# A tile's down weights rounded and split in a step of its own, in a fused attention and mixture-of-experts kernel

## The chip, the cores and the metric

The kernel runs on one core of one Trainium2 chip. The metric is the device time of one execution in microseconds (us), the median of three runs.

## The reference

A cross-attention layer adds its result to `x` (4 batches of 1024 tokens, 256 wide), and then a mixture of 9 experts with 2 experts per token adds its own:

```python
x = x + _L0_xattn_ref(ctx_1024, _layernorm(x, axis=-1), fside_Bx16_0, fside_Bx16_0, ...)
x = x + _L0_ffn_ref(_layernorm(x, axis=-1), L0_ffn_Wr, L0_ffn_Wg, L0_ffn_Wu, L0_ffn_Wd)
```

The second line is the part in question. Each token goes through its two experts, of which each is a gated layer of 704 hidden columns:

```python
gate = jax.nn.silu(jnp.einsum('th,ehi->tei', xf, Wg))
hidden = gate * jnp.einsum('th,ehi->tei', xf, Wu)
out = jnp.einsum('tei,eih,te->th', hidden, Wd, cw)
```

## The kernel before

**Two halves.** Up to about 370 us the attention runs in steps of 128 tokens, and scatters every normalised token to the regions of its two experts in a DRAM table, `expert_in`. Then the experts run in 40 tiles. Tiles 0 to 2 (`EARLY`) are blocks of 256 rows of the expert with most rows. The others are 29 pairs (256 rows) and 8 singles (128 rows, tiles 6, 11, 16, 20, 25, 30, 34 and 39; `SINGLES_AFTER`). A step takes TensorE about 12 us for a pair (10.6 right behind a single) and 9.8 for a single, the down product of the tile before included.

**Split products.** fp32 products are made of three passes (`product`, lines 344 to 346): high part by high part, high by low, low by high. So every operand is split. ScalarE rounds the weights to `wgt_hi` (`round_pieces`, L1122), VectorE subtracts to get `wgt_lo` (`rest_pieces`, L1980). A tile has six pieces of weights (`PIECES`): four of 704 columns for gate and up, and for down one of 1280 columns and one of 256. The same holds for the tokens (`tok_move` L1107, `tok_rest` L1964) and for the hidden values (`hid_round` L1157 to L1160, `hid_rest` L2012 to L2016; for a single L1167 to L1170 and L2024 to L2027). `wgt_hi` and `wgt_lo` have two halves, used by turns.

**A step.** In step t, each engine works off a fixed list:

- TensorE: gate and up of tile t in three units (u = 0, 1, 2) of 256 hidden columns (the last of 192), each into a pair of PSUM banks, used by turns, so unit n waits until VectorE has read unit n-2 (`unit_free`, semaphore `hid_made`). After unit 1 it turns the tokens of tile t+1 (`tok_turn`, L1371), and then makes the down product of tile t-1 (`down`), which waits for the down weights of tile t-1, for its hidden values (`hid_ready`), and for bank space.
- ScalarE, for each unit: `silu`, two pieces of the weights of tile t+1, `hid_round`. After unit 1 also `tok_move(t + 1)` and `res_move(t - 1)`, which empties the down product of the tile before (L1179).
- VectorE, for each unit: `hidden` (gate times up, L1988 to L1991), two pieces of tile t+1, `hid_rest`. After unit 1 also `tok_rest(t + 1)`.

With u = 2 the two pieces are the down weights of tile t+1:

```python
                for u in range(UNITS):
                    hidden(t, u)
                    if t < NT - 1:
                        rest_pieces(t + 1, u, src)
                    hid_rest(t, u)
```

A single has one gate and up (`single_gate_up`), with its 128 tokens as the weights of the array and a hidden result that is turned (`hid_turn`, L1489 to L1492); in its step the four gate and up pieces of tile t+1 and the down product of t-1 all go by, and the down pieces of t+1 come last.

**Loads.** SyncE issues all loads. Pairs' raw weights lie in three slots (`wgt`) that are loaded three pairs ahead and only if the expert changes; a slot's number comes from a table in SBUF by `value_load`. Singles use `spare_wgt`. For each tile it loads the tokens of tile t+1, then refills the down weights behind tile t-1 and the gate and up weights behind tile t, each when VectorE has split the old ones.

**Results.** GpSimd notes the token numbers of tile t+2 (`note`, L930), then adds tile t's result to the output with indirect DMAs (`add_results`, L941), and waits until they have landed.

Of the kernel before, what the change touches and what calls it, by code (L numbers as in the profile page):

```python
# [28 lines left out]
P = 128  # L29
# [85 lines left out]
    return 0 if t < EARLY else t % 2  # L115


def pieces_to(t):

    return (t - EARLY) * len(PIECES)  # L120

def program(nc, x, ctx_rows, fside, ln1_w, ln1_b, ln2_w, ln2_b, wq, wkv, wout, wr, wg, wu, wd, out):
    valmat_dram = nc.dram_tensor("valmat_dram", (B, H, M, DE), F32).ap()
# [2 lines left out]
    with ExitStack() as ctx:  # L126
        def sem(name):
            return ctx.enter_context(nc.semaphore(name))
# [321 lines left out]
        tok_split = sem("tok_split")  # L450
        weights_hi = sem("weights_hi")
        weights_split = sem("weights_split")
        hid_made = sem("hid_made")
        hid_hi = sem("hid_hi")
        pads_zeroed = sem("pads_zeroed")
# [27 lines left out]
        def weights_loaded(t, gate_up):  # L483

            if not is_pair(t):
                return single_gu_loaded if gate_up else single_d_loaded, (TILES[t][1] + 1) * WEIGHT_LOADS
            pair = TILES[t][1]
            return (wgu_loaded if gate_up else wd_loaded)[pair % WEIGHT_SLOTS], (pair // WEIGHT_SLOTS + 1) * WEIGHT_LOADS

        def gate_up_split(t, u):  # L490

            return (early_split, u + 1) if t < EARLY else (weights_split, pieces_to(t) + 2 * KT)

        def down_split(t):
            return (early_split, UNITS + 2) if t < EARLY else (weights_split, pieces_to(t + 1))

        def tokens_loaded(t):
            return tok_loaded[t % 2], (t // 2 + 1) * 16
# [70 lines left out]
        def _(sp):  # L569
# [168 lines left out]
            def refill_gate_up(t):  # L738

                n = TILES[t][1]  # L740
                if is_pair(t) and n + WEIGHT_SLOTS < NP:
                    sp.wait_ge(weights_split, pieces_to(t) + 2 * KT)
                    load_pair_gate_up(n + WEIGHT_SLOTS)
                elif not is_pair(t) and n + 1 < NS:
                    sp.wait_ge(weights_split, pieces_to(t) + 2 * KT)
                    load_single_gate_up(n + 1)

            def refill_down(t):
                n = TILES[t][1]
                if is_pair(t) and n + WEIGHT_SLOTS < NP:  # L750
                    sp.wait_ge(weights_split, pieces_to(t + 1))
                    load_pair_down(n + WEIGHT_SLOTS)
                elif not is_pair(t) and n + 1 < NS:
                    sp.wait_ge(weights_split, pieces_to(t + 1))
                    load_single_down(n + 1)

            for t in range(EARLY, NT):
                if EARLY < t < NT - 1:
                    sp.wait_ge(tok_turned, t)
                    sp.wait_ge(tok_noted, t)  # L760
                    load_tokens(t + 1)
                if t > EARLY:
                    refill_down(t - 1)
                refill_gate_up(t)

            sp.wait_ge(added, BLOCKS_TO[NT] * 16)

# [189 lines left out]
        def _(act):  # L957
# [157 lines left out]

            def round_pieces(t, u, src):

                act.wait_ge(*weights_loaded(t, u < UNITS - 1))
                if u == UNITS - 1 and t > EARLY:
                    act.wait_ge(down_done, t - 1)  # L1120
                for p0, p1 in PIECES[2 * u:2 * u + 2]:
                    nc.scalar.activation(wgt_hi[half_of(t)][:, p0:p1], src[:, p0:p1], ACT.Copy).then_inc(weights_hi, 1)  # L1122

            def early_round(u):

# [56 lines left out]
            def pair_step(t):  # L1182

                ahead = EARLY - 1 <= t < NT - 1
                src = weights_of(t + 1) if ahead else None
                for u in range(UNITS):
                    silu(t, u)
                    if ahead:
                        round_pieces(t + 1, u, src)
                    hid_round(t, u)  # L1190
                    if u == UNITS - 2 and t:
                        tok_move(t + 1)
                        if t == 2:
                            act.wait_ge(last_stored, 16)
                        res_move(t - 1)

            def single_step(t):

                last = t == NT - 1
                src = None if last else weights_of(t + 1)  # L1200
                single_silu(t)
                if not last:
                    round_pieces(t + 1, 0, src)
                    tok_move(t + 1)
                    round_pieces(t + 1, 1, src)
                res_move(t - 1)
                single_hid_round(t)
                if not last:
                    round_pieces(t + 1, 2, src)

            for s in range(T + 4):
                step(s, s)
# [328 lines left out]
        def _(dve):  # L1541
# [431 lines left out]
            def rest_pieces(t, u, src):  # L1973

                i = t % 2
                for n in range(2 * u, 2 * u + 2):
                    p0, p1 = PIECES[n]
                    rows = P if n < len(PIECES) - 1 else FHALF
                    dve.wait_ge(weights_hi, pieces_to(t) + n + 1)
                    nc.vector.tensor_tensor(wgt_lo[i][0:rows, p0:p1], src[0:rows, p0:p1],  # L1980
                                            wgt_hi[i][0:rows, p0:p1].bitcast(F32), ALU.subtract).then_inc(weights_split, 1)

            def hidden(t, u):

# [45 lines left out]
            def pair_step(t):  # L2030

                src = weights_of(t + 1) if t < NT - 1 else None
                for u in range(UNITS):
                    hidden(t, u)
                    if t < NT - 1:
                        rest_pieces(t + 1, u, src)
                    hid_rest(t, u)
                    if t < NT - 1 and u == UNITS - 2:
                        tok_rest(t + 1)

            def single_step(t):

                last = t == NT - 1
                src = None if last else weights_of(t + 1)
                single_hidden(t)
# [61 lines left out]
```

## Time and profile before

| what | value |
|---|---|
| median of 3 runs | 832.52 us (832.21 to 832.76) |
| the profiled execution | 832.81 us, of which the span of its instructions is 831.2 us |
| mean granted TensorE clock | 0.996 |
| TensorE busy | 795.7 us (96%) |
| VectorE, ScalarE, GpSimd busy | 667.6, 625.8, 380.2 us |

The rows below come from the one profiled execution. Times in the timeline count from the start of its span. A row says when an instruction starts, how long it takes, its engine and line, what it writes and reads, and in brackets how long the engine stood idle before it and whose work ended that. Matmuls overlap: the next one starts 0.11 to 0.12 us after a 256-column one that is listed with 0.28 us.

### The profile page before, as it was taken

The page shows a single profiled execution, that of the slowest core. Times are in us where ns is not written, and L with a number is a line of the kernel's source. Part 1 is how long each engine was busy: PE and PEld are TensorE (multiplying, and loading weights), DVE is VectorE, ACT ScalarE, POOL GpSimd, SP SyncE. Part 2 cuts the span into 40 slices and gives each one's busy share as a digit, 9 for nine tenths or more (in the row PEclk, how much of TensorE's full clock was granted, in tenths as well). Part 3 has the DMA queues.
Part 4 walks back from the last instruction along what each step waited for, and adds up shares of the span by engine and source line. Part 5 has one row for each costly group of instructions (what it writes and reads, how often), then busy time and mean ns, then how long its engine had stood idle before and what let it go on. Part 6 is the DMA issues. An engine that isn't in the chain of part 4 may idle for free.

```text
span 831.2 us, 19592 instructions
## 1 busy us (share of the span) xinstructions
PE 795.7 (96%) x6037; PEld 754.9 (91%) x6037; DVE 667.6 (80%) x1620; ACT 625.8 (75%) x1966; POOL 380.2 (46%) x534
## 2 busy tenths in 40 slices
PE   7999999999999999879999999999999999999993
PEld 6866999999999999779999999999999999999993
DVE  6778888888888887887878788787888877888771
ACT  4578898889889888655777778777778777777771
POOL 3021377688778767763334233442343424424232
PEclk9999999999999999999999999999999999999998
DMA  8065900401310020656575182255752654556211
GB/s 288 20 152 147 268 32 30 150 27 40 122 52 33 33 85 27 210 155 171 148 199 120 25 262 46 47 170 152 225 153 46 194 159 119 133 142 160 40 23 23
DMA packets 78044, 96.14 MB, mean 116 GB/s; under 512 B 10680, under 2 KB 65140, under 8 KB 77940
## 3 DMA queue, kind: packets, MB, share of 16 engines
q1 hardware_dynamic: 64179, 75.94, 29.7%
q0 software_dynamic: 13760, 18.96, 12.4%
q8 instruction: 48, 0.79, 0.4%
q14 instruction: 57, 0.46, 0.2%
HBM read 108.14 MB, written 31.29 MB: 168 GB/s over the span
## 4 chain that ended last, share of the span: by engine, by line
PE 82%; DVE 4%; issue 3%; SPq 3%; POOL 2%; DMA 2%; ACT 2%; DVEq 1%; POOLq 0%
PE banks L344 23%; PE banks L345 22%; PE banks L346 22%; PE banks L1357 4%; PE banks L1337 2%; PE banks L1514 2%; PE banks L1371 2%; PE banks L1311 1%; DMA expert_in<-blank 1%; POOL expert_in L878 1%; PE banks L1287 1%; ACT prob L1046 1%; DVEq L1544 1%; PE banks L1323 1%; SPq L657 1%
## 5 line engine op out<-in xcount | busy, mean ns | idle before, releaser
L344 PE MATMUL banks<-tok_t_hi,wgt_hi 128*128 128x256 f32 x704 | 199.7, 284 | 4.8 <-DVE hid_f L1988 1.9
L346 PE MATMUL banks<-tok_t_hi,wgt_lo 128*128 128x256 f32 x704 | 198.0, 281 | 0.0
L345 PE MATMUL banks<-tok_t_lo,wgt_hi 128*128 128x256 f32 x704 | 197.9, 281 | 0.0
L941 POOL DMA_INDIRECT result<-res,tok_id x72 | 117.7, 1635 | 161.2 <-ACT res L1179 129.9
L1046 ACT ACTIVATE prob<-banks,row_min 128x77 f32<-128x77 f32 x512 | 161.8, 375 | 2.9 <-DVE row_min L1711 2.9
L1980 DVE TENSOR_TENSOR wgt_lo<-wgt,wgt_hi 128x704 fp32r<-128x704 f32 x174 | 150.4, 905 | 14.7 <-ACT wgt_hi L1122 14.7
L344 PEld LDWEIGHTS banks<-tok_t_hi,wgt_hi 128*128 128x128 f32 x704 | 134.3, 191 | 7.9 <-issue 5.9
L346 PEld LDWEIGHTS banks<-tok_t_hi,wgt_lo 128*128 128x128 f32 x704 | 133.5, 190 | 0.0
L345 PEld LDWEIGHTS banks<-tok_t_lo,wgt_hi 128*128 128x128 f32 x704 | 133.4, 189 | 0.0
L1122 ACT ACTIVATE wgt_hi<-wgt 128x704 fp32r (+1 forms) x174 | 130.6, 801 | 0.5
L1046 ACT ACTIVATION_READ_ACCUMULATOR prob<-banks,row_min 128x1 f32 x512 | 131.0, 257 | 0.0
L344 PE MATMUL banks<-wgt_hi,hid_hi 128*128 128x256 f32 x360 | 104.3, 290 | 8.7 <-issue 6.1
L346 PE MATMUL banks<-wgt_hi,hid_lo 128*128 128x256 f32 x360 | 101.3, 281 | 0.0
L345 PE MATMUL banks<-wgt_lo,hid_hi 128*128 128x256 f32 x360 | 101.1, 281 | 0.0
L344 PE MATMUL banks<-valmat_hi,prob_t_hi 128*128 128x266 f32 x320 | 94.5, 295 | 1.0 <-DVE logits L1733 1.0
L891 POOL TENSOR_TENSOR prob<-prob,row_inv 128x1232 f32<-128x1232 f32 x32 | 72.1, 2254 | 50.9 <-DVE row_inv L1725 50.9
L345 PE MATMUL banks<-valmat_lo,prob_t_hi 128*128 128x266 f32 x320 | 91.6, 286 | 0.0
L346 PE MATMUL banks<-valmat_hi,prob_t_lo 128*128 128x266 f32 x320 | 91.5, 286 | 0.0
L878 POOL DMA_INDIRECT expert_in<-xn,top_slot x64 | 67.4, 1053 | 39.0 <-POOL xn L868 24.9
L930 POOL COPY tok_gate<-tok 128x2 f32<-128x2 f32 (+1 forms) x40 | 23.9, 598 | 131.8 <-DMA result<-res,tok_id 128.6
L344 PEld LDWEIGHTS banks<-wgt_hi,hid_hi 128*128 128x128 f32 x360 | 68.3, 190 | 10.9 <-DVE wgt_lo L1980 6.0
L1061 ACT ACTIVATE prob_t_hi<-banks 128x512 fp32r<-128x512 f32 (+1 forms) x96 | 48.8, 543 | 33.0 <-PE banks L1357 33.0
(274 smaller groups left out, 2131.3 us busy)
## 6 DMA issues: line engine op xcount, KB each, us to landing
wgt<-in_L_ffn_Wg SPq DMA_DIRECT2D x29, 704.0 KB
wgt<-in_L_ffn_Wu SPq DMA_DIRECT2D x29, 640.0 KB
wgt<-in_L_ffn_Wd SPq DMA_DIRECT2D x29, 640.0 KB
tok<-expert_in SPq DMA_DIRECT2D x32, 258.0 KB, 3.4
spare_wgt<-in_L_ffn_Wg SPq DMA_DIRECT2D x9, 704.0 KB, 4.2
spare_wgt<-in_L_ffn_Wu SPq DMA_DIRECT2D x9, 640.0 KB, 5.9
spare_wgt<-in_L_ffn_Wd SPq DMA_DIRECT2D x9, 640.0 KB, 4.3
valmat_f<-valmat_dram SPq DMA_DIRECT2D x4, 1197.0 KB, 6.3
```

The source lines that it names most:

```text
L344: nc.tensor.matmul(to, a[0], b[0], start=first, stop=False)
L345: nc.tensor.matmul(to, a[0], b[1], start=False, stop=False)
L346: return nc.tensor.matmul(to, a[1], b[0], start=False, stop=last)
L878: nc.gpsimd.indirect_dma_start(expert_in, bass.IndirectOffsetOnAxis(ap=top_slot[c % 4][:, k:k + 1], axis=0), xn[c % 4][:, k, :], None).the ...
L891: nc.gpsimd.tensor_tensor(p, p, row_inv[i][:].unsqueeze(2).to_broadcast([P, H, M]), ALU.mult).then_inc(prob_ready, 1)
L930: nc.gpsimd.tensor_copy(tok_gate[:, t % NOTES, 0:blocks], tok[i][:, 0:blocks, GATE])
L941: nc.gpsimd.indirect_dma_start(out, bass.IndirectOffsetOnAxis(ap=tok_id[:, t % NOTES, a:a + 1], axis=0), res[i][:, a, :], None, compute_op ...
L1046: ins = nc.scalar.activation(prob[c % 2][:, h * M:(h + 1) * M], bank[i][:, (h - h0) * M:(h - h0 + 1) * M], ACT.Exp, bias=row_min[c % 2][:, ...
L1061: ins = nc.scalar.activation(prob_t[c % 2][0][0:rows, m0:m1, :], turned_bank(c, g, rows, m0 - c0, m1 - c0), ACT.Copy)
L1122: nc.scalar.activation(wgt_hi[half_of(t)][:, p0:p1], src[:, p0:p1], ACT.Copy).then_inc(weights_hi, 1)
L1357: mm = nc.tensor.transpose(bank[3 + (c * NG + g) % 2][0:n, (m - c0) * P:(m - c0 + 1) * P], prob[c % 2][:, m * P:m * P + n], ident[:])
L1980: nc.vector.tensor_tensor(wgt_lo[i][0:rows, p0:p1], src[0:rows, p0:p1], wgt_hi[i][0:rows, p0:p1].bitcast(F32), ALU.subtract).then_inc(weig ...
```

## The change

The two down pieces leave `round_pieces` and `rest_pieces`. They get functions of their own, `round_down` and `rest_down`, and semaphores of their own, `down_hi` and `down_split_made`. The down weights of a pair t are now rounded and split in step t, right behind the turned tokens of tile t+1, no longer in step t-1 behind unit 2. For a single t they are made at the end of step t, at the place where those of tile t+1 stood; for the last tile, ahead of its `res_move` and `single_hid_rest`. In exchange, ScalarE and VectorE look up a pair's slot twice, for t+1 and for t. On SyncE the gate and up refill of tile t now comes before the down refill behind tile t-1.

```diff
-def pieces_to(t):
+def gate_pieces_to(t):
-    return (t - EARLY) * len(PIECES)
+    return (t - EARLY) * 2 * KT
+def down_pieces_to(t):
+    return (t - EARLY) * (len(PIECES) - 2 * KT)
...
         def down_split(t):
-            return (early_split, UNITS + 2) if t < EARLY else (weights_split, pieces_to(t + 1))
+            return (early_split, UNITS + 2) if t < EARLY else (down_split_made, down_pieces_to(t + 1))
...
             for t in range(EARLY, NT):
                 if EARLY < t < NT - 1:
                     sp.wait_ge(tok_turned, t)
                     sp.wait_ge(tok_noted, t)
                     load_tokens(t + 1)
+                refill_gate_up(t)
                 if t > EARLY:
                     refill_down(t - 1)
-                refill_gate_up(t)
...
             def round_pieces(t, u, src):
-                act.wait_ge(*weights_loaded(t, u < UNITS - 1))
-                if u == UNITS - 1 and t > EARLY:
-                    act.wait_ge(down_done, t - 1)
+                act.wait_ge(*weights_loaded(t, True))
                 for p0, p1 in PIECES[2 * u:2 * u + 2]:
                     nc.scalar.activation(wgt_hi[half_of(t)][:, p0:p1], src[:, p0:p1], ACT.Copy).then_inc(weights_hi, 1)
+            def round_down(t, src):
+                act.wait_ge(*weights_loaded(t, False))
+                if t > EARLY:
+                    act.wait_ge(down_done, t - 1)
+                for p0, p1 in PIECES[2 * KT:]:
+                    nc.scalar.activation(wgt_hi[half_of(t)][:, p0:p1], src[:, p0:p1], ACT.Copy).then_inc(down_hi, 1)
...
                 src = weights_of(t + 1) if ahead else None
+                own = weights_of(t) if t >= EARLY else None
                 for u in range(UNITS):
                     silu(t, u)
-                    if ahead:
+                    if ahead and u < UNITS - 1:
                         round_pieces(t + 1, u, src)
                     hid_round(t, u)
                     if u == UNITS - 2 and t:
                         tok_move(t + 1)
+                        if t >= EARLY:
+                            round_down(t, own)
                         if t == 2:
                             act.wait_ge(last_stored, 16)
                         res_move(t - 1)
...
+                if last:
+                    round_down(t, spare_wgt[:])
                 res_move(t - 1)
                 single_hid_round(t)
                 if not last:
-                    round_pieces(t + 1, 2, src)
+                    round_down(t, spare_wgt[:])
...
+            def rest_down(t, src):
+                i = t % 2
+                for n, (p0, p1) in enumerate(PIECES[2 * KT:]):
+                    rows = FHALF if n else P
+                    dve.wait_ge(down_hi, down_pieces_to(t) + n + 1)
                     nc.vector.tensor_tensor(wgt_lo[i][0:rows, p0:p1], src[0:rows, p0:p1],
-                                            wgt_hi[i][0:rows, p0:p1].bitcast(F32), ALU.subtract).then_inc(weights_split, 1)
+                                            wgt_hi[i][0:rows, p0:p1].bitcast(F32), ALU.subtract).then_inc(down_split_made, 1)
...
                 for u in range(UNITS):
                     hidden(t, u)
-                    if t < NT - 1:
+                    if t < NT - 1 and u < UNITS - 1:
                         rest_pieces(t + 1, u, src)
                     hid_rest(t, u)
-                    if t < NT - 1 and u == UNITS - 2:
-                        tok_rest(t + 1)
+                    if u == UNITS - 2:
+                        if t < NT - 1:
+                            tok_rest(t + 1)
+                        if t >= EARLY:
+                            rest_down(t, own)
...
+                if last:
+                    rest_down(t, spare_wgt[:])
                 single_hid_rest(t)
                 if not last:
-                    rest_pieces(t + 1, 2, src)
+                    rest_down(t, spare_wgt[:])
```

VectorE's list in the first pair step whose next tile is a single, from the turned tokens of the single to the first products of its hidden values. Before (`L1980` are the down pieces of the single, `L2015` and `L2016` are `hid_rest` of the pair's unit 2, `L1971` is the look-up of a slot):

```order
L1964 TENSOR_TENSOR tok_t_lo<-banks,tok_t_hi 128x2x128 [waits tok_moved]
L1990 TENSOR_TENSOR hid_f<-gate_act,banks 128x256 [waits silu_done]
L1991 TENSOR_TENSOR hid_f<-gate_act,banks 64x256
L1980 TENSOR_TENSOR wgt_lo<-spare_wgt,wgt_hi 128x1280 [waits weights_hi]
L1980 TENSOR_TENSOR wgt_lo<-spare_wgt,wgt_hi 64x256 [waits weights_hi]
L2015 TENSOR_TENSOR hid_lo<-hid_f,hid_hi 128x256 [waits hid_hi]
L2016 TENSOR_TENSOR hid_hi<-hid_f,hid_hi 64x256
L1971 TENSOR_LOAD tile_table
L1971 ISA x2
L2000 TENSOR_TENSOR single_hid<-single_act,banks 128x256 [waits silu_done]
L2001 TENSOR_TENSOR single_hid<-single_act,banks 128x64
```

Now (`L2005` are the down pieces of the pair itself, its `ISA` rows compute the slot's address, `L2040` and `L2041` are `hid_rest`, and `L1988` is the look-up):

```order
L1981 TENSOR_TENSOR tok_t_lo<-banks,tok_t_hi 128x2x128 [waits tok_moved]
L2005 ISA [waits down_hi]
L2005 TENSOR_TENSOR wgt_lo<-wgt,wgt_hi 128x1280
L2005 ISA [waits down_hi]
L2005 TENSOR_TENSOR wgt_lo<-wgt,wgt_hi 64x256
L2015 TENSOR_TENSOR hid_f<-gate_act,banks 128x256 [waits silu_done]
L2016 TENSOR_TENSOR hid_f<-gate_act,banks 64x256
L2040 TENSOR_TENSOR hid_lo<-hid_f,hid_hi 128x256 [waits hid_hi]
L2041 TENSOR_TENSOR hid_hi<-hid_f,hid_hi 64x256
L1988 TENSOR_LOAD tile_table
L1988 ISA x2
L2025 TENSOR_TENSOR single_hid<-single_act,banks 128x256 [waits silu_done]
```

The two down pieces have moved from between `hidden` and `hid_rest` of unit 2 to ahead of that `hidden`; `hid_rest` now follows `hidden` directly.

ScalarE's list at the same place. Before (`L1122` are the down pieces of the single, `L1179` empties the down product of the tile before, `L1146` and `L1147` are `silu` of unit 2, `L1159` and `L1160` are `hid_round`):

```order
L1107 ACTIVATE tok_t_hi<-banks 128x2x128 [waits tok_turned]
L1179 ACTIVATE res<-banks,tok_gate 128x256 [waits added,tok_noted,down_done]
L1179 ACTIVATE res<-banks,tok_gate 128x256
L1146 ACTIVATE gate_act<-banks 128x256 [waits gu_done]
L1147 ACTIVATE gate_act<-banks 64x256
L1122 ACTIVATE wgt_hi<-spare_wgt 128x1280 [waits down_done,single_d_loaded]
L1122 ACTIVATE wgt_hi<-spare_wgt 128x256
L1159 ACTIVATE hid_hi<-hid_f 128x256 [waits hid_made]
L1160 ACTIVATE hid_hi<-hid_f 64x256
```

Now (`L1134` are the down pieces of the pair itself, `L1191` empties the down product):

```order
L1113 ACTIVATE tok_t_hi<-banks 128x2x128 [waits tok_turned]
L1134 ISA [waits down_done,wd_loaded2]
L1134 ACTIVATE wgt_hi<-wgt 128x1280
L1134 ISA
L1134 ACTIVATE wgt_hi<-wgt 128x256
L1191 ACTIVATE res<-banks,tok_gate 128x256 [waits added,tok_noted,down_done]
L1191 ACTIVATE res<-banks,tok_gate 128x256
L1158 ACTIVATE gate_act<-banks 128x256 [waits gu_done]
L1159 ACTIVATE gate_act<-banks 64x256
L1171 ACTIVATE hid_hi<-hid_f 128x256 [waits hid_made]
L1172 ACTIVATE hid_hi<-hid_f 64x256
```

The rounding of the down pieces has moved from between `silu` and `hid_round` of unit 2 to between the turned tokens and the emptying of the down product. TensorE's list has not changed.

## Rows read from the trace of the kernel before

**Rows 1.** The page, busy time, share of the span, instructions
```profile
PE 795.7 (96%) x6037; PEld 754.9 (91%) x6037; DVE 667.6 (80%) x1620; ACT 625.8 (75%) x1966; POOL 380.2 (46%) x534
```

**Rows 2.** Waits, 400 to 831 us: total us, times, longest
```profile
PEld banks L344 <- DVE wgt_lo L1980: 7.0, 12, 1.3
PE banks L344 <- issue: 6.8, 11, 2.0
```

**Rows 3.** Timeline, TensorE, start of down products in single steps
```profile
436.19 0.35 PE L344 MATMUL banks<-wgt_hi,hid_hi 128*128 128x256 f32 x1 [0.59 <-issue]
...
492.18 0.60 PE L1371 MATMUL banks<-ident,tok 128*128 128x128 f32 x4
493.34 0.36 PE L344 MATMUL banks<-wgt_hi,hid_hi 128*128 128x256 f32 x1 [0.56 <-issue]
...
811.20 0.36 PE L344 MATMUL banks<-wgt_hi,hid_hi 128*128 128x256 f32 x1 [0.99 <-DVE wgt_lo L1980]
```

**Rows 4.** Timeline, VectorE, around the second single
```profile
486.86 0.42 DVE L1964 TENSOR_TENSOR tok_t_lo<-banks,tok_t_hi 128x256 fp32r<-128x256 f32 x1
489.34 0.42 DVE L1990 TENSOR_TENSOR hid_f<-gate_act,banks 128x256 f32<-128x256 f32 x1 [2.07 <-ACT gate_act L1147]
489.78 0.42 DVE L1991 TENSOR_TENSOR hid_f<-gate_act,banks 64x256 f32<-64x256 f32 x1
490.64 1.82 DVE L1980 TENSOR_TENSOR wgt_lo<-spare_wgt,wgt_hi 128x1280 fp32r<-128x1280 f32 x2 [0.45 <-ACT wgt_hi L1122]
...
492.82 0.42 DVE L2016 TENSOR_TENSOR hid_hi<-hid_f,hid_hi 64x256 fp32r<-64x256 f32 x1
...
496.41 1.68 DVE L1980 TENSOR_TENSOR wgt_lo<-wgt,wgt_hi 128x704 fp32r<-128x704 f32 x2
```

**Rows 5.** Timeline, ScalarE, around the second single
```profile
485.31 0.36 ACT L1107 ACTIVATE tok_t_hi<-banks 128x256 fp32r<-128x256 f32 x1
486.39 0.84 ACT L1179 ACTIVATE res<-banks,tok_gate 128x256 f32<-128x256 f32 x2 [0.72 <-PE banks L1514]
488.53 0.39 ACT L1146 ACTIVATE gate_act<-banks 128x256 f32<-128x256 f32 x1 [1.31 <-PE banks L346]
...
489.33 1.59 ACT L1122 ACTIVATE wgt_hi<-spare_wgt 128x1280 fp32r<-128x1280 f32 x2
...
491.13 0.41 ACT L1160 ACTIVATE hid_hi<-hid_f 64x256 fp32r<-64x256 f32 x1
```

**Rows 6.** Timeline, the pair step after the first single, by engine
```profile
443.39 1.82 DVE L1980 TENSOR_TENSOR wgt_lo<-wgt,wgt_hi 128x1280 fp32r<-128x1280 f32 x2 [0.39 <-ACT wgt_hi L1122]
445.14 0.67 DVE L1988 TENSOR_TENSOR hid_f<-gate_act,banks 128x512 f32<-128x512 f32 x1
...
450.75 0.67 DVE L1964 TENSOR_TENSOR tok_t_lo<-banks,tok_t_hi 128x512 fp32r<-128x512 f32 x1
...
452.58 0.42 DVE L1991 TENSOR_TENSOR hid_f<-gate_act,banks 64x256 f32<-64x256 f32 x1
...
449.66 0.47 ACT L1179 ACTIVATE res<-banks,tok_gate 128x256 f32<-128x256 f32 x1
451.34 0.39 ACT L1146 ACTIVATE gate_act<-banks 128x256 f32<-128x256 f32 x1 [1.21 <-PE banks L346]
...
451.52 0.35 PE L344 MATMUL banks<-tok_t_hi,wgt_hi 128*128 128x256 f32 x1 [0.22 <-issue]
```

**Rows 7.** Line L1971, VectorE's look-up of a slot: ns min/median/max, first and last start
```profile
L1971 DVEq TENSOR_LOAD <-tile_table x28: 300/304/550, 396.8 to 785.0; - x28
L1971 DVEq FUSED_REGOPS  x28: 190/190/216, 397.4 to 785.4; - x28
```

**Rows 8.** Timeline, the end: GpSimd adds the result of tile 38
```profile
817.18 1.56 POOL L941 DMA_INDIRECT result<-res,tok_id  x1 [7.88 <-ACT res L1179]
```

**Rows 9.** Timeline, tokens: TensorE waits for a tile's; SyncE issues a later one's
```profile
412.48 0.66 PE L1371 MATMUL banks<-ident,tok 128*128 128x128 f32 x4 [0.31 <-DMA tok<-expert_in]
...
502.40 0.39 SPq L668 DMA_DIRECT2D tok<-expert_in  x1
```

More of the change, by code:

```diff
@@ L452, in program @@
         weights_split = sem("weights_split")
+        down_hi = sem("down_hi")
+        down_split_made = sem("down_split_made")
         hid_made = sem("hid_made")
@@ L490, in gate_up_split @@
         def gate_up_split(t, u):
-            return (early_split, u + 1) if t < EARLY else (weights_split, pieces_to(t) + 2 * KT)
+            return (early_split, u + 1) if t < EARLY else (weights_split, gate_pieces_to(t + 1))
         def down_split(t):
-            return (early_split, UNITS + 2) if t < EARLY else (weights_split, pieces_to(t + 1))
+            return (early_split, UNITS + 2) if t < EARLY else (down_split_made, down_pieces_to(t + 1))
         def tokens_loaded(t):
@@ L741, in refill_gate_up @@
                 if is_pair(t) and n + WEIGHT_SLOTS < NP:
-                    sp.wait_ge(weights_split, pieces_to(t) + 2 * KT)
+                    sp.wait_ge(weights_split, gate_pieces_to(t + 1))
                     load_pair_gate_up(n + WEIGHT_SLOTS)
                 elif not is_pair(t) and n + 1 < NS:
-                    sp.wait_ge(weights_split, pieces_to(t) + 2 * KT)
+                    sp.wait_ge(weights_split, gate_pieces_to(t + 1))
                     load_single_gate_up(n + 1)
@@ L750, in refill_down @@
                 if is_pair(t) and n + WEIGHT_SLOTS < NP:
-                    sp.wait_ge(weights_split, pieces_to(t + 1))
+                    sp.wait_ge(down_split_made, down_pieces_to(t + 1))
                     load_pair_down(n + WEIGHT_SLOTS)
                 elif not is_pair(t) and n + 1 < NS:
-                    sp.wait_ge(weights_split, pieces_to(t + 1))
+                    sp.wait_ge(down_split_made, down_pieces_to(t + 1))
                     load_single_down(n + 1)
@@ L1977, in rest_pieces @@
                     p0, p1 = PIECES[n]
-                    rows = P if n < len(PIECES) - 1 else FHALF
-                    dve.wait_ge(weights_hi, pieces_to(t) + n + 1)
+                    dve.wait_ge(weights_hi, gate_pieces_to(t) + n + 1)
+                    nc.vector.tensor_tensor(wgt_lo[i][:, p0:p1], src[:, p0:p1], wgt_hi[i][:, p0:p1].bitcast(F32), ALU.subtract
+                                            ).then_inc(weights_split, 1)
+            def rest_down(t, src):
[3 more added lines that the diff above has]
+                    dve.wait_ge(down_hi, down_pieces_to(t) + n + 1)
                     nc.vector.tensor_tensor(wgt_lo[i][0:rows, p0:p1], src[0:rows, p0:p1],
-                                            wgt_hi[i][0:rows, p0:p1].bitcast(F32), ALU.subtract).then_inc(weights_split, 1)
+                                            wgt_hi[i][0:rows, p0:p1].bitcast(F32), ALU.subtract).then_inc(down_split_made, 1)
             def hidden(t, u):
@@ L2032, in pair_step @@
                 src = weights_of(t + 1) if t < NT - 1 else None
+                own = weights_of(t) if t >= EARLY else None
                 for u in range(UNITS):
                     hidden(t, u)
-                    if t < NT - 1:
+                    if t < NT - 1 and u < UNITS - 1:
                         rest_pieces(t + 1, u, src)
                     hid_rest(t, u)
-                    if t < NT - 1 and u == UNITS - 2:
-                        tok_rest(t + 1)
+                    if u == UNITS - 2:
[3 more added lines that the diff above has]
+                            rest_down(t, own)
             def single_step(t):
```

## The prediction

> **What bounds the kernel now.** First the page: TensorE is busy for 96% of the span [rows 1], and at full clock, so only its gaps can be won, unless work leaves it, and none does. Then the waits of the expert half, where all edits lie: TensorE's own waits for VectorE's weight pieces and "issue" come to 7.0 us in front of weight loads and 6.8 us in front of matmuls [rows 2]. The two count the same gaps twice, so some 8 us is all there is. Then the timeline of TensorE, to see where the gaps are. In plain pair steps there is none. In each of the 8 single steps the down product of the pair before starts late: 0.59 us idle at 436.19, 0.56 at 493.34, 0.99 at 811.20 [rows 3]; the other five (550, 595, 652, 709, 754) show 0.56 once and 0.59 four times. Measured from start to start it is 0.16 more, since a matmul is listed 0.28 us long where the next starts after 0.12: the four turned-token matmuls at 492.18 take 4 x 0.11 us, so the down product was due at 492.62, and came at 493.34, 0.72 late [rows 3].
>
> Who ends that wait? The view names the weights or "issue". The down product waits for its weights (made a step earlier), bank space (long free), and the pair's last hidden values. VectorE's list shows the third: `hidden` of unit 2 is done at 489.78 + 0.42 = 490.20, then the two down pieces of the single run from 490.64, and only then `hid_rest` ends at 492.82 + 0.42 = 493.24, 0.10 before TensorE starts [rows 4]. So VectorE does 1.75 us of work for a later product, after 0.45 of waiting for ScalarE's rounding, ahead of what TensorE wants now.
>
> **The change part by part.** *Taken out from between `hidden` and `hid_rest`: two subtractions on VectorE and two roundings on ScalarE.* ScalarE may round the hidden values when `hidden` is done at 490.20. Its two instructions took from about 490.8 to 491.13 + 0.41 [rows 5], some 0.7 us, so they end near 490.95, and `hid_rest`'s two (0.86 us, [rows 4]) near 491.9. TensorE comes at 492.62. Margin 0.7 us: the wait goes whole. Seven times 0.74 (0.56 to 0.59 plus 0.16) is 5.2 us, the last one 0.99 + 0.16 = 1.15. **Sum 6.3 us.** Behind the last one, GpSimd's adds start from ScalarE's emptying of that very down product [rows 8], so the end of the span moves with it.
>
> *Put in, behind the turned tokens.* VectorE stands idle for 2.07 us there, from 487.28 to `hidden` at 489.34 [rows 4]; the two pieces fill 1.75 of it. ScalarE has two holes, 0.72 before it empties the down product and 1.31 before unit 2's `silu` [rows 5]; the roundings (1.5 us) fit into 2.03, though the emptying starts some 0.8 later, for which only GpSimd's adds wait (TensorE needs that bank a step later). I cost this at nothing. If the cover were gone, `hidden` of unit 2 would slip, and TensorE's unit 1 of the next step waits for it, one unit (2.9 us) after the end of unit 2.
>
> *The step behind a single is the tight one,* since VectorE has no hole: from the down pieces at 443.39 to the turned tokens at 450.75 + 0.67 it is busy, and TensorE waits for these, 0.22 idle at 451.52 [rows 6]. The change leaves that chain as it is: it starts from the end of the down product, and as many pieces of the same sizes lie in it. So TensorE cannot win there what it saves elsewhere in the same step, and this gap stays. Behind the tokens, the down pieces now run from 451.35 to 453.10, and `hidden` of unit 2 ends at about 453.95, where it was 452.58 + 0.42 = 453.00 [rows 6]. TensorE's next unit 1 is due 24 matmuls x 0.12 after 451.52, at 454.4. Margin 0.4 us: nothing lost. If it slips further, seven steps pay.
>
> *The second look-up of a slot,* in 28 pair steps on ScalarE and on VectorE. One is a load of 0.30 and register work of 0.19, from 785.0 to about 785.6, so 0.6 us of the sequencer [rows 7]. It runs while the engine still works off what it was given. In plain steps there is room. Behind a single it must fit beside the down pieces: two look-ups, 1.2 us, against the 1.75 us from 443.39 to 445.14 [rows 6]. Bounds: nothing, or all of it in seven steps, 7 x 0.6 = 4.2 us. I take nothing, by the room of 1.75.
> The Trainium skill, page "DMA: Bandwidth & Descriptors", section "Latency and other measured facts", gives a `tensor_load` a floor of about 0.6 us. With that figure two look-ups would take 1.8 us, and together with the hand-over of the pieces some 0.3 us would show in each of seven steps, an estimate of 2.1 us given back, so 828.3 us. The trace has 0.30 [rows 7] and does not agree, and I go by the trace.
>
> *SyncE.* Its list is as long as before. The down refill now waits for pieces made later, and the tokens of the tile after next stand behind both refills. Around a single they were issued at 502.40 [rows 9]; I expect 3 us later. They are needed by TensorE's turn at about 514, two steps on. If they came late, it would look as at 412.48, 0.31 us idle [rows 9]; that one, before the first changed refill, stays. Cost nothing. The loads of weights are needed three pairs later, as before.
>
> **Sum.** Own time 832.81 us less 6.3 is 826.5. The profiled execution lies 0.29 over the median, so the median should come to **826.2 us**. No more than 0.2% (1.7 us) apart counts as no change.
>
> **Rivals.**
> 1. *Part is given back behind the singles.* The emptier list shows new waits: the look-ups (up to 4.2 us), or unit 1's wait for `hidden` of unit 2, whose margin of 0.4 us is made of estimates; each 0.3 us over it costs 7 x 0.3 = 2.1. For it: VectorE is saturated there. Against: both have rows with room. Time 828 to 830.5. The floor for a load on the page of the Trainium skill named above ("DMA: Bandwidth & Descriptors") is this rival's case of 828.3 us; of its chance I give that 0.03, since 28 loads of 0.30 speak against it.
> 2. *The gap isn't the hidden values'.* "Issue" in [rows 3] could be TensorE's own, when it turns to other weights. Then nothing moves: 832.5. Against: the start follows `hid_rest` by 0.10 us, and where no turned tokens come before (811.20) the gap is longer by just their 0.4.
> 3. *Slower: `hidden` of unit 2 becomes late in every pair step.* The place is VectorE's hole behind the turned tokens. The down pieces now stand ahead of `hidden` and wait for ScalarE's rounding and for the loaded weights. Their room is the 2.07 us hole and 1.2 us more: unit 1 is due 2.9 us after unit 2's end, of which `silu` takes 0.8 and `hidden` 0.86. Beyond that TensorE waits in each of 28 steps. It decides from 3.3 us on, against 1.75 measured [rows 4]. At 3.8 us it would cost 28 x 0.5 = 14 us, less the 6.3: 840. Against: it needs the pieces to take twice their time.
> 4. *More is won.* If the gaps behind singles (0.22 idle, [rows 6], up to 0.38 from start to start, seven of them) went too, some 2 us more: 824.
>
> **How the numbers follow.** Forecast (825.4 to 827.2) 0.72, rival 1 0.11, rival 2 0.05, rival 3 0.05, rival 4 0.07. The likeliest gives 826.2. The range goes down to 824.8, for part of rival 4 and my 0.2 us a step, and up to 829.2, for most of rival 1; what is left out is rivals 2 and 3, the end of rival 1 and half of rival 4, under 0.2. Faster by over 0.2% is the forecast, rival 4 and nearly all of rival 1: 0.89, and I take off a little for what I have not thought of: 0.87. Within 0.2%: 0.07. Slower: 0.06.
>
> **What would show it.** In the profile after: TensorE's down product follows the turned tokens in single steps without a gap, all eight times; VectorE's `hid_rest` directly behind `hidden` and ScalarE's rounding; the two down pieces in VectorE's hole behind the turned tokens, and the idle time before `hidden` of unit 2 (2.07) down to about 0.3; the emptying of the down product about 0.8 us later than TensorE's end; the gap of 0.2 behind singles still there; tokens issued 3 us later without a wait on them. The prediction is wrong if a gap stays in front of the down product, if TensorE waits in front of unit 1 in plain pair steps, or if the look-ups show as idle time before unit 0's `silu` or `hidden` with TensorE behind them.

## The result, and the profile after

The changed kernel takes 825.71 us, median of 4 executions (825.07 to 826.43), where the kernel before took 832.52. The ratio is 0.9918 (95% interval 0.9906 to 0.993): 6.8 us less, where 6.3 were forecast. The profiled execution took 826.43 us with a span of 824.8 (before: 831.2).

The page of the changed kernel, busy time and share of the span, answers to [rows 1]:

```profile
PE 792.2 (96%) x6037; PEld 755.3 (92%) x6037; DVE 670.0 (81%) x1620; ACT 625.4 (76%) x1966; POOL 382.7 (46%) x534
```

The counts of instructions are the same, so no engine does less work; only gaps went. TensorE's busy time is 3.5 us less all the same, because a matmul is listed 0.28 us long where the next one can start after 0.12: the first part of each gap counts as busy. The waits of the changed kernel, 400 to 825 us (engine, line waited for: us in total, times, longest), answer to [rows 2]:

```profile
DVE hid_f L2015 <- ACT gate_act L1159: 23.6, 22, 1.3
DVE hid_lo L2040 <- ACT hid_hi L1172: 23.0, 29, 0.8
...
PEld banks L348 <- issue: 5.6, 8, 2.3
...
PE banks L348 <- issue: 4.1, 7, 2.0
```

The wait for `wgt_lo` in front of a product has left the list. Of the 4.1 us, 2.0 is the very last down product's. Where the rest is, TensorE's timeline shows (L1388 turns tokens, L1506 to L1509 turn a single's hidden values, L348 begins a product; it answers to [rows 3], [rows 6] and [rows 9]):

```profile
412.77 0.60 PE L1388 MATMUL banks<-ident,tok 128*128 128x128 f32 x4
...
450.85 0.35 PE L348 MATMUL banks<-tok_t_hi,wgt_hi 128*128 128x256 f32 x1 [0.29 <-issue]
...
491.50 0.60 PE L1388 MATMUL banks<-ident,tok 128*128 128x128 f32 x4
491.85 0.36 PE L348 MATMUL banks<-wgt_hi,hid_hi 128*128 128x256 f32 x1
...
496.55 0.27 PE L1509 MATMUL banks<-ident,single_hid 128*64 128x128 f32 x1
496.58 0.36 PE L348 MATMUL banks<-tok_t_hi,wgt_hi 128*128 128x256 f32 x1
```

The down product at 491.85 starts 0.35 us after the token turn at 491.50, where it took 493.34 - 492.18 = 1.16 [rows 3]. All eight of these gaps are gone. Another gain was not forecast. From the turn of a single's hidden values to the next gate product TensorE took 0.74 us five times and 0.65 twice before, now 0.57 to 0.59 each time, 1.0 us over seven singles. The gaps behind the singles grew: from start to start 0.38, 0.18, 0.38, 0.18, 0.18, 0.38, 0.19 (1.9 us) became 0.45, 0.17, 0.72, 0.47, 0.39, 0.56, 0.48 (3.2 us). The gaps in front of the down products were 5.8 us over seven singles and 1.1 at the last, so the balance is 5.8 + 1.1 + 1.0 - 1.4 = 6.5 us. A count without any model of gaps gives 6.7: from the turn of tile 5's tokens to the start of the last down product, TensorE takes 405.7 us before (412.48 to 818.20) and 399.0 now (412.77 to 811.74). The whole span is only 6.4 us shorter, since the changed kernel's profiled execution was already 0.8 us late at a token turn at 343.29 (before: 342.49), ahead of every changed step; 0.5 of that came back, as it did not have the token wait of [rows 9].

VectorE in the changed kernel around the second single (L2005 are the two down pieces, L2015 and L2016 `hidden` of unit 2, L2040 and L2041 `hid_rest`, L1996 pieces of the next tile's gate and up weights), to lay beside [rows 4]:

```profile
485.01 0.42 DVE L1981 TENSOR_TENSOR tok_t_lo<-banks,tok_t_hi 128x256 fp32r<-128x256 f32 x1
485.57 1.82 DVE L2005 TENSOR_TENSOR wgt_lo<-wgt,wgt_hi 128x1280 fp32r<-128x1280 f32 x2
488.66 0.42 DVE L2015 TENSOR_TENSOR hid_f<-gate_act,banks 128x256 f32<-128x256 f32 x1 [1.27 <-ACT gate_act L1159]
489.10 0.42 DVE L2016 TENSOR_TENSOR hid_f<-gate_act,banks 64x256 f32<-64x256 f32 x1
490.31 0.42 DVE L2040 TENSOR_TENSOR hid_lo<-hid_f,hid_hi 128x256 fp32r<-128x256 f32 x1 [0.79 <-ACT hid_hi L1172]
490.75 0.42 DVE L2041 TENSOR_TENSOR hid_hi<-hid_f,hid_hi 64x256 fp32r<-64x256 f32 x1
...
494.59 1.68 DVE L1996 TENSOR_TENSOR wgt_lo<-wgt,wgt_hi 128x704 fp32r<-128x704 f32 x2
```

And ScalarE there (L1134 rounds the down pieces, L1191 empties the down product), beside [rows 5]:

```profile
484.13 1.58 ACT L1134 ACTIVATE wgt_hi<-wgt 128x1280 fp32r x2
485.71 0.84 ACT L1191 ACTIVATE res<-banks,tok_gate 128x256 f32<-128x256 f32 x2
487.86 0.39 ACT L1158 ACTIVATE gate_act<-banks 128x256 f32<-128x256 f32 x1 [1.31 <-PE banks L350]
...
489.55 0.42 ACT L1171 ACTIVATE hid_hi<-hid_f 128x256 fp32r<-128x256 f32 x1 [0.92 <-DVE hid_f L2016]
```

The hidden values are ready at 490.75 + 0.42 = 491.17, 0.68 us ahead of the product. Both engines now wait in front of `hid_rest` for each other's previous step instead of working on weights.

### The profile page after: what moved, and what is told of

Its sections match the earlier page's. It is cut to its first block, busy times and chain, and to the rows that moved or that the text cites. A ratio compares the mean times of both kernels' runs of the same rounds, so it can differ in the third digit from the quotient of the medians.

```text
span 824.8 us, 19760 instructions
## 1 busy us (share of the span) xinstructions
PE 792.2 (96%) x6037; PEld 755.3 (92%) x6037; DVE 670.0 (81%) x1620; ACT 625.4 (76%) x1966; POOL 382.7 (46%) x534
## 4 chain that ended last, share of the span: by engine, by line
PE 87%; DVE 5%; ACT 2%; issue 1%; DVEq 1%; POOL 1%; DMA 1%; SPq 0%; POOLq 0%
PE banks L348 25%; PE banks L349 24%; PE banks L350 24%; PE banks L1374 4%; PE banks L1354 2%; PE banks L1531 2%; PE banks L1388 2%; PE banks L1328 1%; DVEq L1561 1%; PE banks L1304 1%; ACT prob L1052 1%; PE banks L1340 1%; DMA wkv_sb<-in_L_xattn_Wkv 0%; DMA result<-res,tok_id 0%; DVE prob_t_lo L1703 0%
## 5 line engine op out<-in xcount | busy, mean ns | idle before, releaser
L348 PE MATMUL banks<-tok_t_hi,wgt_hi 128*128 128x256 f32 x704 | 200.3, 285 | 5.1 <-issue 2.5
L947 POOL DMA_INDIRECT result<-res,tok_id x72 | 119.4, 1658 | 144.9 <-ACT res L1191 111.6
L348 PEld LDWEIGHTS banks<-tok_t_hi,wgt_hi 128*128 128x128 f32 x704 | 135.0, 192 | 6.9 <-issue 6.0
L348 PE MATMUL banks<-wgt_hi,hid_hi 128*128 128x256 f32 x360 | 104.2, 290 | 3.5 <-issue 2.0
L1996 DVE TENSOR_TENSOR wgt_lo<-wgt,wgt_hi 128x704 fp32r<-128x704 f32 x116 | 97.8, 884 | 0.6 <-issue 0.2
L348 PE MATMUL banks<-valmat_hi,prob_t_hi 128*128 128x266 f32 x320 | 94.4, 295 | 0.9 <-DVE logits L1750 0.9
L1126 ACT ACTIVATE wgt_hi<-wgt 128x704 fp32r (+1 forms) x116 | 84.9, 784 | 0.0
L936 POOL COPY tok_gate<-tok 128x2 f32<-128x2 f32 (+1 forms) x40 | 20.6, 515 | 138.4 <-DMA result<-res,tok_id 138.4
L348 PE MATMUL banks<-keymat_hi,zn_t_hi 128*128 128x462 f32 (+1 forms) x192 | 72.7, 379 | 0.0
```

The costliest lines, as they stand in the source:

```text
L348: nc.tensor.matmul(to, a[0], b[0], start=first, stop=False)
L936: nc.gpsimd.tensor_copy(tok_gate[:, t % NOTES, 0:blocks], tok[i][:, 0:blocks, GATE])
L947: nc.gpsimd.indirect_dma_start(out, bass.IndirectOffsetOnAxis(ap=tok_id[:, t % NOTES, a:a + 1], axis=0), res[i][:, a, :], None, compute_op ...
L1996: nc.vector.tensor_tensor(wgt_lo[i][:, p0:p1], src[:, p0:p1], wgt_hi[i][:, p0:p1].bitcast(F32), ALU.subtract).then_inc(weights_split, 1)
```

## The experiments

The theory: the down product waited for `hid_rest`, which stood behind the pieces. Its rivals: the gap belongs to TensorE; or the gain has another source in the change. x1 to x4 ran beside 15 executions of the kernel before (median 832.61), x5 to x8 beside 12 (832.71). Ratios are to those.

**x1_put_back.** The changed kernel with everything as it is (functions, semaphores, two look-ups, the refill order), but a pair's own down pieces made between `silu` and `hid_round`, and between `hidden` and `hid_rest`, of its unit 2:

```diff
+                    if t >= EARLY and u == UNITS - 1:
+                        round_down(t, own)
                     hid_round(t, u)
...
-                        if t >= EARLY:
-                            round_down(t, own)
...
+                    if t >= EARLY and u == UNITS - 1:
+                        rest_down(t, own)
                     hid_rest(t, u)
...
-                        if t >= EARLY:
-                            rest_down(t, own)
```

> The changed kernel, with the down pieces of a pair's own tile put back between `hidden` and `hid_rest` of unit 2 (VectorE) and between `silu` and `hid_round` (ScalarE); own semaphores, second look-up and the new refill order stay. Theory (the gain is the hidden values' wait in single steps): the gap in front of the down product comes back eight times, 0.7 to 0.8 us each and 1.2 at the last, so 832 us, within 1 us of the kernel before (832.52). Rival (the gain comes from the new refill order or the semaphores): it stays near 825.7.

Measured: 833.9 us (11 executions), ratio 1.0016 (1.0007 to 1.0025). The whole gain is gone, with 1.3 us more. Timeline of x1, VectorE's down pieces and TensorE's down products:

```profile
433.89 1.82 DVE L2005 TENSOR_TENSOR wgt_lo<-wgt,wgt_hi 128x1280 fp32r<-128x1280 f32 x2 [0.56 <-ACT wgt_hi L1134]
...
436.58 0.36 PE L348 MATMUL banks<-wgt_hi,hid_hi 128*128 128x256 f32 x1 [0.71 <-issue]
...
812.90 0.36 PE L348 MATMUL banks<-wgt_hi,hid_hi 128*128 128x256 f32 x1 [1.11 <-DVE wgt_lo L2005]
```

All eight gaps are back, each 0.12 us longer than before (0.71 for 0.59, 1.11 for 0.99, [rows 3]); VectorE waits 0.56 us for the rounding where it waited 0.45 [rows 4]. That is 1.0 of the 1.3 us. So the place of the pieces carries the gain; the rest of the change brings none by itself. That the extra 0.11 is the slot's address, which both engines now work out here, was not measured apart.

**x2_rounding_moved_only.** From the changed kernel; ScalarE rounds early as in the change, VectorE still splits between `hidden` and `hid_rest`:

```diff
+                    if t >= EARLY and u == UNITS - 1:
+                        rest_down(t, own)
                     hid_rest(t, u)
...
-                        if t >= EARLY:
-                            rest_down(t, own)
```

> ScalarE rounds the down pieces at the new place, VectorE subtracts them at the old one, ahead of `hid_rest`. Theory: VectorE no longer waits 0.45 us for the rounding, but its 1.75 us of work still lie ahead, so `hid_rest` ends some 0.3 us after the down product is due (0.7 at the last): gaps of 0.3 x 7 + 0.7 = 2.8 us, 828.5 us. Rival (VectorE's wait for ScalarE was the cost): all of the gain stays, 825.7.

Measured: 829.14 us (5 executions), ratio 0.9963 (0.9949 to 0.9976), about half of the gain. Timeline of x2, VectorE around the second single, then two of TensorE's down products:

```profile
488.81 1.82 DVE L2005 TENSOR_TENSOR wgt_lo<-wgt,wgt_hi 128x1280 fp32r<-128x1280 f32 x2
490.55 0.41 DVE L2040 TENSOR_TENSOR hid_lo<-hid_f,hid_hi 128x256 fp32r<-128x256 f32 x1
...
434.86 0.35 PE L348 MATMUL banks<-wgt_hi,hid_hi 128*128 128x256 f32 x1 [0.18 <-issue]
...
807.11 0.36 PE L348 MATMUL banks<-wgt_hi,hid_hi 128*128 128x256 f32 x1 [0.57 <-issue]
```

VectorE's wait of 0.45 us for the rounding is gone, and the seven gaps shrink from 0.59 idle to 0.18, the last from 0.99 to 0.57, 0.42 each: 3.3 us, close to the 3.5 measured. The other half needs VectorE's own 1.75 us out of the way, and so does the 1.0 us at the next gate product: from the turn of a single's hidden values to that product TensorE takes 0.74 us five times and 0.65 twice in x2, as before. It also speaks against the rival that the gap is TensorE's own: TensorE's list is the same in x1, x2 and the change, and the gap has three sizes.

**x5_hidden_first.** From the kernel *before*: nothing leaves its step; only the order within unit 2 is turned, `hid_round` and `hid_rest` ahead of the pieces.

```diff
-                    if ahead:
+                    if ahead and u < UNITS - 1:
                         round_pieces(t + 1, u, src)
                     hid_round(t, u)
+                    if ahead and u == UNITS - 1:
+                        round_pieces(t + 1, u, src)
...
-                    if t < NT - 1:
+                    if t < NT - 1 and u < UNITS - 1:
                         rest_pieces(t + 1, u, src)
                     hid_rest(t, u)
+                    if t < NT - 1 and u == UNITS - 1:
+                        rest_pieces(t + 1, u, src)
```

> The kernel before, with only this turned round in unit 2 of a pair step: `hid_round` and `hid_rest` come first, then the two down pieces of the next tile. Theory: the gap in front of the down product goes, but VectorE then does the 1.75 us of pieces ahead of the single's own products and pieces, so gate and up of the tile behind the single waits instead (some 1 us in each of seven); the gain is lost there but for the last single: 832.5 us, within 1 us. Rival (whatever gets the pieces out of the way of `hid_rest` gives the whole gain): 826.

Measured: 835.19 us (8 executions), ratio 1.0031 (1.002 to 1.0041): slower than before, though the gap that the prediction was about is gone. Timeline of x5, VectorE and then TensorE (L1982 are weight pieces, L2017 is `hid_rest`, L1373 turns tokens):

```profile
491.41 0.43 DVE L2017 TENSOR_TENSOR hid_lo<-hid_f,hid_hi 128x256 fp32r<-128x256 f32 x1 [0.79 <-ACT hid_hi L1160]
...
492.57 1.82 DVE L1982 TENSOR_TENSOR wgt_lo<-spare_wgt,wgt_hi 128x1280 fp32r<-128x1280 f32 x2 [0.31 <-ACT wgt_hi L1122]
...
497.56 1.68 DVE L1982 TENSOR_TENSOR wgt_lo<-wgt,wgt_hi 128x704 fp32r<-128x704 f32 x2
...
492.59 0.60 PE L1373 MATMUL banks<-ident,tok 128*128 128x128 f32 x4
492.95 0.36 PE L344 MATMUL banks<-wgt_hi,hid_hi 128*128 128x256 f32 x1
...
499.30 0.39 PE L344 MATMUL banks<-tok_t_hi,wgt_hi 128*128 128x256 f32 x1 [1.38 <-DVE wgt_lo L1982]
```

The down product starts on time (0.36 after the turn), and TensorE stands 1.38 us in front of the next tile's gate product, for weight pieces that end at 497.56 + 1.68 = 499.24. It does so in all seven singles that a pair follows, 1.38 to 1.49 us each, 10.2 in all. The kernel before had this limit too, hidden by the first gap. Its timeline of TensorE:

```profile
498.03 0.27 PE L1492 MATMUL banks<-ident,single_hid 128*64 128x128 f32 x1
498.14 0.39 PE L344 MATMUL banks<-tok_t_hi,wgt_hi 128*128 128x256 f32 x1
```

The pieces it needs ended at 496.41 + 1.68 = 498.09 [rows 4], 0.05 ahead of it, and in the other six singles the distance is the same. So VectorE's list from `hidden` of unit 2 to the last gate piece set the pace of the single step, with the gap only showing where. In x5 that list is longer by its waits, 0.79 + 0.31 for 0.45: from the start of `hidden` to the end of the pieces 9.48 us (489.76 to 499.24) for 8.75 (489.34 to 498.09). The changed kernel has 494.59 + 1.68 - 488.66 = 7.61, as the down pieces no longer lie in it. The expectation had the place of the stall right and its size too small.

**x3_one_lookup.** From the changed kernel; the slot's number that step t-1 read for t is kept, not read again:

```diff
+            looked_up = {}
...
-                src = weights_of(t + 1) if ahead else None
-                own = weights_of(t) if t >= EARLY else None
+                own = looked_up.get(t)
+                src = looked_up[t + 1] = weights_of(t + 1) if ahead else None
...
-                src = None if last else weights_of(t + 1)
+                src = looked_up[t + 1] = None if last else weights_of(t + 1)
```

> The changed kernel with one look-up of a slot per step: the register of the step before is used again. Theory (look-ups are mostly covered): VectorE shows 0.19 us of 'issue' in front of unit 0's `hidden` behind one single, and the gaps behind singles grew by 1.4 us in all, of which 1.0 is TensorE's earlier arrival; so 0.4 us less than the changed kernel, a ratio to before of about 0.9913. Rival (a load's floor of about 0.6 us, as a page of the notes gives it): 2 us less, ratio 0.9895.

Measured: 824.93 us (5 executions), ratio 0.9911 (0.9897 to 0.9924), against 0.9913 (0.99 to 0.9927) of the changed kernel run again (x8): not told apart by the times. The trace does tell: the gaps behind singles sum to 2.6 us from start to start (0.45, 0.17, 0.44, 0.44, 0.18, 0.44, 0.47), for 3.2 in the changed kernel. By this the second look-up costs some 0.6 us (0.5 against x8, whose gaps sum to 3.1). Its rows in the changed kernel (VectorE's sequencer, then ScalarE's; min/median/max in ns) and the one place where it shows in front of VectorE's `hidden` of unit 0:

```profile
L1988 DVEq TENSOR_LOAD <-tile_table x56: 298/306/659, 397.0 to 791.5; - x56
```

```profile
L1120 ACTq TENSOR_LOAD <-tile_table x56: 272/280/602, 396.3 to 790.8; - x56
```

```profile
557.21 0.69 DVE L2013 TENSOR_TENSOR hid_f<-gate_act,banks 128x512 f32<-128x512 f32 x1 [0.19 <-issue]
```

The median load is 0.31 us. The floor of about 0.6 us in the Trainium skill ("DMA: Bandwidth & Descriptors", "Latency and other measured facts") is reached by three of VectorE's 56 loads and one of ScalarE's 56, so the measured median decides; the case of 828.3 us that rested on it did not come.

**x4_single_early.** From the changed kernel; in single steps too the down pieces are made ahead of `res_move` and `single_hid_round`, and on VectorE ahead of `single_hid_rest`, as the change does for the last tile alone:

```diff
-                if last:
-                    round_down(t, spare_wgt[:])
+                round_down(t, spare_wgt[:])
                 res_move(t - 1)
                 single_hid_round(t)
-                if not last:
-                    round_down(t, spare_wgt[:])
...
-                if last:
-                    rest_down(t, spare_wgt[:])
+                rest_down(t, spare_wgt[:])
                 single_hid_rest(t)
-                if not last:
-                    rest_down(t, spare_wgt[:])
```

> The changed kernel; in every single step (not only the last) the single's own down pieces come ahead of the emptying of the down product and of `single_hid_rest`, in the time in which ScalarE (1.54 us) and VectorE (1.03 us) wait for TensorE. Theory (TensorE's gap behind singles is VectorE's chain from there to the turned tokens): VectorE is 0.5 us earlier at unit 0's `hidden`, the seven gaps of 0.17 to 0.72 us (3.2 in all) shrink to under 0.3 in all, and the time is 822.8 us, ratio 0.988. Rival (the gap is set by ScalarE or by the tokens' turn): no change, 825.7.

Measured: 822.99 us (4 executions), ratio 0.9886 (0.9871 to 0.9901). Timeline of x4, VectorE in the first single step (L2002 are the single's down pieces, L2046 is `single_hid_rest`):

```profile
439.29 1.81 DVE L2002 TENSOR_TENSOR wgt_lo<-spare_wgt,wgt_hi 128x1280 fp32r<-128x1280 f32 x2
441.02 0.68 DVE L2046 TENSOR_TENSOR hid_lo<-banks,hid_hi 128x512 fp32r<-128x512 f32 x1
...
443.18 0.69 DVE L2010 TENSOR_TENSOR hid_f<-gate_act,banks 128x512 f32<-128x512 f32 x1 [0.99 <-ACT gate_act L1156]
```

VectorE now waits 0.99 us for the next unit 0, where it came late, and none of TensorE's starts behind a single is later by more than 0.12. The gap behind singles is the same kind of gap as the first: weights for later, standing ahead of what is wanted now.

**x6_old_refill_order.** From the changed kernel, with the down refill again ahead of the gate and up refill:

```diff
-                refill_gate_up(t)
                 if t > EARLY:
                     refill_down(t - 1)
+                refill_gate_up(t)
```

> The changed kernel with the refills in the old order (down behind tile t-1 first, then gate and up behind tile t). Theory: loads have two or three steps of room, so no change: 825.7, within 0.5 us. Rival (the order matters): over 1 us slower.

Measured: 827.05 us (5 executions, 826.96 to 827.61), ratio 0.9934 (0.9921 to 0.9948), where x8 beside it took 825.65 (825.19 to 825.72): 1.4 us slower. That is the rival's case ("over 1 us slower"), not the theory's. Timeline of x6, SyncE's loads and TensorE's turn:

```profile
657.99 0.37 SPq L661 DMA_DIRECT2D spare_wgt<-in_L_ffn_Wd  x1
...
661.81 0.39 SPq L654 DMA_DIRECT2D wgt<-in_L_ffn_Wg  x1
...
664.87 0.38 SPq L674 DMA_DIRECT2D tok<-expert_in  x1
...
670.29 0.66 PE L1388 MATMUL banks<-ident,tok 128*128 128x128 f32 x4 [1.02 <-DMA tok<-expert_in]
```

And the same place in x8, the changed kernel:

```profile
654.25 0.39 SPq L654 DMA_DIRECT2D wgt<-in_L_ffn_Wg  x1
...
657.56 0.38 SPq L661 DMA_DIRECT2D spare_wgt<-in_L_ffn_Wd  x1
...
660.54 0.39 SPq L674 DMA_DIRECT2D tok<-expert_in  x1
...
668.86 0.60 PE L1388 MATMUL banks<-ident,tok 128*128 128x128 f32 x4
```

In both, the down refill waits until the down pieces are split (in x6 they end at 657.25). The gate and up loads were through before that in x8; in x6 they stand behind it, and the tokens behind them go out 4.3 us later and land after TensorE asks for them: 1.02 us idle here. With a second, smaller one at 569.15 it is 1.4 us from start to start. From tile 5's turn to the last down product TensorE takes 400.1 us in x6 and 398.8 in x8. So the refill order is no ornament: with pieces made later, the old order would give back 1.4 us.

**x7_both**, x3 and x4 together, and **x8_changed_again**, the changed kernel as it is:

> x4_single_early and x3_one_lookup together. In x4's trace only four gaps of 0.11 us are left behind singles, so the look-ups have nothing left to cost: 0 to 0.5 us under x4, 822.5 to 823.0. If look-ups cost time elsewhere too: 822.2 or less.

> The changed kernel itself, on the same chip as the three others: 825.7, within 0.5 us.

Measured: x7 822.61 us (4 executions), ratio 0.988 (0.9865 to 0.9895); x8 825.65. x7 has the lowest time of all, 3.0 us under the change and 10.1 under the kernel before. It is not told apart from x4 by the times. Behind its singles no gap is listed.

## Why the prediction was right, and where it was not

- *Which gap, and who ends it: right.* x1 brings all eight gaps back by the place of the pieces alone, x2 splits them into the wait for the rounding and VectorE's own work.
- *The sum, 7 x 0.74 + 1.15 = 6.3: a little small.* The start-to-start excess was 0.81 to 0.83 each, because the four token turns take 0.35 us when nothing waits (491.50 to 491.85), not 4 x 0.11. That is 5.8 us, not 5.2. The last gave its 1.1. That 6.3 lies so near the measured 6.8 is in part luck: the gaps that the sum names gave 6.9, and two terms that it does not have, 1.0 us won and 1.4 lost, nearly cancel.
- *The down product's wait as the single step's only limit: wrong, and it was not seen.* TensorE won 1.0 us at the next gate product, since it had been held there too, 0.05 us behind VectorE's pieces in all seven. Had the change merely turned the order in unit 2, that reasoning would have promised 6 us, and x5 measured 2.5 us slower. It held here because the change takes 1.75 us of VectorE's work out of the stretch and not only behind `hid_rest`.
- *The gap behind singles stays: its place right, its size not.* It grew by 1.4 us. 0.6 of that is the second look-up (x3). The rest fits the row it stood on: VectorE's chain runs from the down product's end, so the 1.0 us that TensorE saved in front of it comes back as waiting. That part was argued, not tested.
- *The pieces behind the turned tokens cost nothing: right, with more room than forecast.* Idle time before `hidden` of unit 2 is 1.27 us, not 0.3. VectorE reached the tokens 3.65 us ahead of that `hidden` (485.01 to 488.66), where it was 2.48 (486.86 to 489.34). In the step behind a single, `hidden` of unit 2 ends at 452.82 + 0.42 = 453.24 in a kernel that runs 0.7 earlier there, as forecast, and TensorE's next unit waits for nothing. Rival 3 had no case. The emptying of the down product does not come 0.8 us late either: it starts at 485.71, 0.04 behind TensorE's end at 485.67, since ScalarE reached the tokens 1.4 us earlier (483.87 for 485.31).
- *The look-ups cost nothing: not quite.* They cost 0.6 of at most 4.2 us, and one of the prediction's own signs of being wrong is there once: VectorE stands 0.19 us in front of `hidden` of unit 0 at 557.21, and TensorE's gap behind it, at 563.61, is 0.72 us, where x3 has 0.44. ScalarE stands idle in front of a `silu` twice (0.37 us at 510.70, 0.38 at 667.55), which it does not in x3, but no wait of TensorE follows.
- *SyncE, cost nothing: right for the change, with less room than stated.* Around the second single the tokens go out at 504.20, 1.8 us later than before [rows 9] and not 3, for a turn at 512.90; further on they go out 8 us ahead of their turn, and x6 shows that 4 us less are too few. That the wait at 412.48 [rows 9] stays was wrong: at 412.77 there is none, nor in x2 to x4, x7 and x8. x1 and x5 have it (0.44 and 0.43 us idle) and x6 has 0.16. What decides it was not tested.
- *The end moves with the last pair's down product: right.* Between the start of GpSimd's add for it and the end of the span lie 14.0 us before (817.18 to 831.2) and 14.1 now (810.72 to 824.8).

## What to carry to other kernels

In an engine's list, work for later that stands between two steps of what TensorE wants next is paid as far as it outlasts TensorE's other work (here 0.83 us of 2.20 each time, 0.45 of waiting and 1.75 of work). The same work in front of the first step, where the engine waits anyway, cost nothing here. Before trusting the first gap, look for the second limit right behind it: a start within 0.1 us of its producer's end, with no idle time listed, can become the next wait as soon as the gap closes. When a buffer's release is moved later, its refill belongs behind the loads that are wanted sooner, in the list that issues both: the other order cost 1.4 us here (x6).

## What the runs showed of the hardware that was not expected

TensorE's granted clock fell in the last down product in four of the ten traced executions (x2, x6, x7, x8) and not in the others, one of them of the same kernel as x8. The stretches of that product, x8 and then the changed kernel's profiled execution (us, busy time of PE, PEld, DVE, ACT, POOL, granted clock, DMA share, GB/s):

```profile
810.80:814.40 3.60, 3.56 (x17) 3.50 (x17) 0.00 (x0) 0.00 (x0) 2.13 (x2) 0.54 0.51 49
```

```profile
811.70:814.00 2.30, 2.24 (x17) 2.06 (x17) 0.00 (x0) 0.00 (x0) 2.00 (x2) 1.00 0.47 57
```

At 0.54, nearly all of it runs at the lower of the two levels (1.2 of 2.4 GHz). It follows 2.03 us in which TensorE stood still for the last hidden values, which all of these kernels have. The 17 matmuls, 0.21 us apart instead of 0.12, take 3.35 us from the first start to the last where the changed kernel's take 1.97; in x2, x7 and x6, where the clock fell at other places of the product, they take 3.30, 2.72 and 2.41. The end of the span does not notice: GpSimd's last add waits for the transfers of the adds before it, not for this product. It starts at 815.90 in x8, 6.08 us after the add at 809.82, and in the changed kernel 6.01 after the pair's first add, in GpSimd's timeline (it answers to [rows 8]):

```profile
810.72 1.56 POOL L947 DMA_INDIRECT result<-res,tok_id  x1 [6.64 <-ACT res L1191]
...
816.73 1.56 POOL L947 DMA_INDIRECT result<-res,tok_id  x1 [2.59 <-DMA result<-res,tok_id]
```

So a trace may show a product at half clock beside an unchanged time. If the last product set the end, it would be up to 1.4 us of scatter (an estimate, 3.35 less 1.97).

Some of GpSimd's small casts are listed up to ten times longer beside VectorE's subtractions. The changed kernel, GpSimd and VectorE:

```profile
563.31 0.19 POOL L936 COPY tok_gate<-tok 128x2 f32<-128x2 f32 x1 [5.18 <-DMA result<-res,tok_id]
563.43 1.85 POOL L937 CAST tok_id<-tok 128x2 int32<-128x2 f32 x1
```

```profile
563.43 1.81 DVE L2005 TENSOR_TENSOR wgt_lo<-wgt,wgt_hi 128x1280 fp32r<-128x1280 f32 x2
```

The cast of 128x2 numbers, 0.18 us at its shortest, is listed from 563.43 to 565.28, and the two subtractions from SBUF beside it from 563.43 to 565.24. The Trainium skill ("SBUF — State Buffer", "SBUF: two separate sides") says of VectorE and GpSimd that a VectorE operation with two SBUF inputs and a GpSimd one that reads SBUF shut each other out for a whole instruction. The rows agree on GpSimd's side: the cast ends 0.04 us behind the second subtraction. No run here tests it the other way round. It is off the path here, since only the adds follow.
